# First chunk of a fused transformer block: keys formed ahead of values, values summed on GpSimd, and a new work order

## The chip, the cores and the metric

One NeuronCore of one Trainium2 chip runs one launch of the kernel. The metric is the device time of that launch in microseconds (us). The engines are named as the profile names them: PE (TensorE, matrix products; PEld is its weight load), DVE (VectorE), ACT (ScalarE), POOL (GpSimd) and SP (SyncE, which issues most DMAs).

## The reference

An input x of 2048 tokens by 256 features goes through three residual branches: half a top-1 gated attention, a gated linear recurrence with a skip matrix, and half the same attention again (same weights).

```python
def _L0_ffn_ref(x, W_gate, W_qkv):          # used twice, on _layernorm(x)
    gating = jax.nn.softmax(x @ W_gate.T, axis=-1)          # 16 heads
    idx = jnp.argmax(gating, axis=-1)
    indicator = jax.nn.one_hot(idx, H, dtype=gating.dtype)
    gating_top1 = indicator * jnp.max(gating, axis=-1, keepdims=True)
    q, k, v = jnp.split(x @ W_qkv.T, 3, axis=-1)
    k_shared = jnp.einsum('bth,bthd->btd', indicator, k)    # one key of 16 per token
    v_shared = jnp.einsum('bth,bthd->btd', gating_top1, v)  # one value of 16 per token
    att = jnp.einsum('bhqd,bkd->bhqk', q, k_shared) * (1.0 / math.sqrt(hd))
    att = softmax(causal(att))
    return jnp.einsum('bhqk,bkd->bhqd', att, v_shared)      # 16 heads
x = x + 0.5 * _L0_ffn_ref(_layernorm(x), ...)
x = x + _L0_attn_ref(_layernorm(x), ...)    # gates, a scan over time, W_out, W_skip
x = x + 0.5 * _L0_ffn_ref(_layernorm(x), ...)
```

## The kernel before

**Tiling.** The 2048 tokens are four chunks of 512 tokens (four tiles of 128). An attention *unit* is one layer, one chunk of queries and one group of four heads: 32 units in all, 320 *steps* of one key tile each. In a step PE forms the scores of four heads against 128 keys (`qk`, L1703), ACT takes the exponential (L1191), POOL masks the diagonal tile (L911), and PE multiplies with the shared values (`pv`, L1715). Before a unit may start, the largest score of each query is needed. It is found apart: PE forms the scores the other way round in *maximum banks* (`max`, L1680), DVE or ACT reduce them (L1406, L1409, L1175), POOL joins them (L930 to L933), PE turns the result into a row (`row`, L1671), ACT evicts it and SP sends it into the query tile by DMA (L830).

**Side work.** For each chunk a list named `prepare` gives the layer norm (`stats` on DVE, `norm` on POOL), the turned tokens (`turn`), the gate scores (`gate`), the top-1 choice (`pick`), the query products (`q`, sent through DRAM by `qout` and `qin`), key and value products (`kv`) and their sum over the chosen head (`choose`), the packed keys (`kpack`), their transposes (`keys`), and differences of keys (`dpack`, `dkeys`). The recurrence branch and the splitting of weights into two f16 parts (`bias`, `size`, `scale`, `split`) are side work too.

**First chunk.** For chunk 0 of layer 0, DVE multiplies each 128x512 bank of keys and values with the pick (L1370) and reduces it over the heads (L1377). Four such pairs, then ACT copies the values (L1122) and packs the keys (L1124), POOL finishes the packing (L969, L970), and PE transposes (L1627). In the other chunks POOL sums the products by halving (L955, L957).

**Order.** Each engine runs its part of one list, `ORDER`, in that order, and semaphores do the rest. The list begins with `FIRST_WORK`, written out; after that a string of digits, `PICKS`, says which of six queues gives the next item (scores, sums, maxima, ends, rows, side work). The string was found by a search over a planner, the class `Clock`, whose constants `WEIGHT`, `KEEPS` and others cost each item. A letter in the string is a group of *spare matmuls*: products of a constant whose result nobody reads (L1518 into a free bank, L1521 adding zeros to the sums), there to keep TensorE active. PE takes one of eight PSUM banks for each item and waits until its last reader is done (`bank_free`).

Of the kernel before, what the change touches and what calls it, by code (L numbers as in the profile page):

```python
# [142 lines left out]
def branch(c):  # L143
# [18 lines left out]
RINGED = {"weights", "scale", "wgate", "range", "bias", "turn", "gate", "kv", "q", "keys", "gates", "skip", "rec", "fin", "row", "max",  # L162
# [6 lines left out]
    "bias": (400, [("DVE", 200), ("POOL", 3500)]),  # L169
# [21 lines left out]
STRETCH, KEEPS, WAKES = 3413.3, 1843.0, 1480.0  # L191
# [12 lines left out]
def weights(e, past):  # L204
# [59 lines left out]
class Clock:  # L264
# [155 lines left out]
    "5522222222222255225255542255020252225055012222050422a525522220100111202225340221205150022122051122201002214223",  # L420
    "22221112023022222020222210220122221112222224322220020522022222222010220122201100221540010201025011202223500122",
    "202255555511510550222n0b01202b22022102201222222515122222452225553022555550225225222205500025005222210010115514",
    "02220152202212022252211022223202225522201022a52220102201522022101200221222252055555022154222222112222020555022",
    "32220525522201220205122020122015220220102220102202102222010220142022221220222122220211222022230220010202202102",
    "02211022201202201202220102220140222012222012222222102222022112202023020102022015005511022120220120220120222010",
    "222014202222120502212222a5222221100223220555222220122220522012220102120502212222050221022201220502505222220122",
    "05220412022252201022212202215122220530220122522201022021102022102220515500102022102225012022012205222201200252",
    "22100222120202142220522555022552205522202122550221122222252003122001220112222050221002210202215522500212220a50",
    "20522120022155005120222102201205502214202222522221202555222221122222225552023022052025255222201500225050022510",
# [122 lines left out]
def macaron_block(nc, x, gamma, beta, w_in, b_in, w_out, b_out, w_skip, b_skip, w_gate, w_qkv, out):  # L552
# [6 lines left out]
    with ctx:  # L559
# [1205 lines left out]
```

## Time and profile before

| | before |
|---|---|
| median of 3 runs | 843.93 us (842.96 to 843.97) |
| time of the profiled execution | 842.89 us |
| its span, first to last instruction | 841.2 us |
| PE busy | 805.8 us, 96% |
| DVE busy | 732.1 us, 87% |
| ACT busy | 710.9 us, 85% |
| POOL busy | 307.4 us, 37% |
| mean granted TensorE clock | 0.984 of full speed |

The profiled execution took 842.89 us, 1.7 us more than its span; the rest is around the first and the last instruction. Busy time is the union of an engine's records. Matmuls overlap in the record, so a busy PE need not be at its peak. The granted clock is 1.00 at 2.4 GHz and 0.50 at 1.2 GHz.

### The profile page before, as it was taken

The numbers are of one execution on the slowest core, as the hardware profiler recorded it, in microseconds if no ns is written. First come the engines' busy times: TensorE is split into PE (matmuls) and PEld (weight loads), VectorE is DVE, ScalarE is ACT, GpSimd is POOL, SyncE is SP. The second block draws the span as 40 slices with busy tenths as digits, with TensorE's granted clock in tenths as the row PEclk, the third lists the DMA queues.
The fourth block names the chain that finished last, engine by engine and source line by source line (L and its number), as shares of the span: only waits on it lengthen the run. The fifth ranks groups of instructions, "written<-read, shape, count | busy, mean of one in ns | idle before, by whom it ended". The sixth has DMA issues, their size and how long they took to land.

```text
span 841.2 us, 18837 instructions
## 1 busy us (share of the span) xinstructions
PE 805.8 (96%) x6403; PEld 283.5 (34%) x6403; DVE 732.1 (87%) x2315; ACT 710.9 (85%) x1117; POOL 307.4 (37%) x600
## 2 busy tenths in 40 slices
PE   8999899999999999999999999999999999999997
PEld 6433433333223332324333443332223333222221
DVE  5889799899999999999749996999999899999810
ACT  1149697979999899797989998899988998999996
POOL 3236424733113433246546258441234353011010
PEclk9999699999999999999999999999999999999999
DMA  6110000101000000200020001000001100000000
GB/s 191 61 59 7 2 2 20 47 14 53 2 2 2 1 2 2 64 1 2 2 64 2 2 12 54 3 1 26 3 2 34 33 27 27 2 2 2 1 1 26
DMA packets 20253, 17.99 MB, mean 21 GB/s; under 512 B 4144, under 2 KB 20160, under 8 KB 20160
## 3 DMA queue, kind: packets, MB, share of 16 engines
q1 hardware_dynamic: 19072, 15.74, 6.2%
q8 instruction: 52, 0.85, 0.4%
q10 hardware_dynamic: 1088, 1.07, 0.4%
q14 instruction: 41, 0.34, 0.1%
HBM read 10.24 MB, written 6.29 MB: 20 GB/s over the span
## 4 chain that ended last, share of the span: by engine, by line
PE 65%; DVE 13%; ACT 12%; issue 8%; POOL 1%; DMA 1%; SPq 0%; POOLq 0%; ACTq 0%; DVEq 0%
PE ps L1715 22%; PE ps L1680 14%; PE ps L1703 12%; ACT probs L1191 8%; DVE ps L1409 7%; ACT relu L1175 3%; PE ps L1598 3%; DVE mxp L1406 2%; PE ps L1646 2%; PE ps L1613 2%; DVE mxp L1409 1%; PE ps L1603 1%; PE ps L1653 1%; PE ps L1570 1%; PE ps L1618 1%
## 5 line engine op out<-in xcount | busy, mean ns | idle before, releaser
L1191 ACT ACTIVATE probs<-ps 128x1024 f32<-128x1024 f32 (+4 forms) x750 | 545.9, 807 | 53.7 <-PE ps L1703 49.1
L1715 PE MATMUL ps<-probs,v_l 128*32 128x512 f32 (+3 forms) x2560 | 298.5, 546 | 2.4 <-POOL probs L911 1.7
L1406 DVE TENSOR_REDUCE mxp<-ps 128x1 f32<-128x512 f32 x384 | 240.9, 684 | 9.8 <-PE ps L1680 5.9
L1409 DVE CUSTOM_DVE_ANT_0 ps<-ps,mask 128x384 f32<-128x384 f32 (+3 forms) x512 | 233.4, 525 | 15.7 <-PE ps L1680 14.7
L1703 PE MATMUL ps<-q_t,k_tl 50*128 50x512 f16 (+3 forms) x1280 | 225.6, 353 | 13.5 <-DMA q_t<-m_row 4.2
L1680 PE MATMUL ps<-k_tl,q_t 48*128 48x512 f16 (+3 forms) x1152 | 224.5, 336 | 4.4 <-DVE mxp L1409 1.2
L911 POOL TENSOR_SCALAR_AFFINE_SELECT probs<-probs 128x256 f32<-128x256 f32 (+1 forms) x192 | 91.7, 488 | 209.7 <-ACT probs L1191 208.6
L1409 DVE CUSTOM_DVE_ANT_0 ps<-ps,relu 128x256 f32<-128x256 f32 (+1 forms) x256 | 136.2, 587 | 8.1 <-PE ps L1680 7.0
L1680 PEld LDWEIGHTS ps<-k_tl,q_t 48*128 48x128 f16 x1152 | 70.5, 94 | 153.1 <-DVE mxp L1406 46.5
L1703 PEld LDWEIGHTS ps<-q_t,k_tl 50*128 50x128 f16 x1280 | 61.9, 94 | 175.2 <-ACT probs L1191 90.8
L1175 ACT ACTIVATE relu<-ps 128x512 f32<-128x512 f32 x192 | 107.3, 626 | 8.5 <-PE ps L1680 7.8
L1409 DVE DVE_READ_ACCUMULATOR2_ANT mxp<- 128x1 f32 x768 | 108.3, 141 | 0.0
L1715 PEld LDWEIGHTS ps<-probs,v_l 128*32 128x32 f32 x2560 | 53.6, 108 | 88.4 <-issue 74.4
L930 POOL TENSOR_SCALAR mxs<-mxf 128x16 f32<-128x16 f32 x32 | 8.1, 254 | 143.1 <-DVE mxf L1419 142.9
L917 POOL TENSOR_TENSOR x_sb<-x_sb,y_att 128x256 f32<-128x256 f32 x32 | 23.4, 730 | 54.6 <-DVE y_att L1432 54.3
L955 POOL TENSOR_TENSOR prod<-prod 128x512 f32<-128x512 f32 (+2 forms) x42 | 34.5, 820 | 22.7 <-DVE prod L1370 20.5
L1428 DVE RECIPROCAL rec<-ps 128x16 f32<-128x16 f32 x32 | 8.1, 252 | 39.8 <-PE ps L1689 39.8
L1680 PE MATMUL ps<-kd_tl,q_t 48*128 48x512 f16 x128 | 36.4, 382 | 1.8 <-DVE mxp L1409 1.0
L1598 PE MATMUL ps<-wqkv_x,ut_x 128*128 128x512 f16 x144 | 34.6, 380 | 0.1
L1370 DVE TENSOR_TENSOR prod<-ps,pick 128x512 f32<-128x512 f32 x32 | 22.0, 686 | 5.2 <-PE ps L1598 3.8
L876 POOL TENSOR_SCALAR u<-x_sb,rstd,shift 128x256 f32<-128x256 f32 x48 | 26.0, 555 | 1.1
L865 POOL TENSOR_TENSOR rstd<-var,half 128x4 f32<-128x4 f32 x12 | 12.5, 1038 | 35.2 <-DVE neg L1255 35.2
(183 smaller groups left out, 633.6 us busy)
## 6 DMA issues: line engine op xcount, KB each, us to landing
q_t<-q_scratch SPq DMA_DIRECT2D x96, 64.0 KB, 2.2
q_scratch<-q_part SPq DMA_DIRECT2D x16, 256.0 KB, 2.2
out_dram<-x_sb SPq DMA_DIRECT2D x4, 512.0 KB, 3.2
x_sb<-in_L_attn_x_dram SPq DMA_DIRECT2D x3, 512.0 KB, 5.1
q_t<-m_row SPq DMA_DIRECT2D x64, 4.0 KB
wqkv_n<-in_L_ffn_W_qkv_dram ACTq DMA_DIRECT2D x1, 768.0 KB, 5.7
w_in_sb<-in_L_attn_W_in_dram SPq DMA_DIRECT2D x1, 384.0 KB, 5.5
x_sb<-in_L_attn_x_dram ACTq DMA_DIRECT2D x1, 256.0 KB, 3.7
```

Source lines behind the costliest of these rows:

```text
L876: last = g_.tensor_scalar(u[:, t, :], x_sb[:, TC * c + t, :], rstd[:, t:t + 1], shift[:, t:t + 1], ALU.mult, ALU.add)
L911: g_.affine_select(out=pr, in_=pr, compare_op=ALU.is_ge, fill=0.0, base=0, pattern=[[0, n], [1, P]], channel_multiplier=-1).then_inc(s_msk, 1)
L917: g_.tensor_tensor(xs, xs, y_att[:, :, :].rearrange("p (i h) d -> p i (h d)", h=GH), op=ALU.add).then_inc(s_xa, 1)
L955: own(g_.tensor_tensor(pairs[:, :, 0:m], pairs[:, :, 0:m], pairs[:, :, m:2 * m], op=ALU.add))
L1175: a_.activation(relu[:, n % RELU_BUFS, :], bank_of(e), ACT.Relu).then_inc(s_ra, 1)
L1191: last = a_.activation(out[:, done:done + banks], scores, ACT.Exp, scale=SCALE / LIFT ** 2)
L1406: last = v_.tensor_reduce(to, scores, axis=AX, op=ALU.max)
L1409: last = v_.tensor_tensor_reduce(scores, scores, added, 1.0, LOWEST, ALU.add, ALU.max, accum_out=to)
L1598: last = mm(bank[:, :], ut_x[:, dc, a, t * P:(t + 1) * P], wqkv_x[:, b, dc, D:3 * D], start=n == 0, stop=n == 3 * DC - 1)
L1680: last = mm(bank[:, col:col + w], q_rows(ROWS_X, c, g, hh, i * P, P), keys, start=True, stop=True)
L1703: last = mm(ps[:, BANK[e][n % 2], col:col + w], k_cols(ROWS_XM, hh, l, kt, P), q_rows(ROWS_XM, c, g, hh, P * i, QW - P * i), start=True, s ...
L1715: last = mm(out_bank[VW * hh:VW * hh + VW, P * i:QW], v_l[:, l, kt, :], probs[:, s % NB, hh, P * i:QW], start=j == 0, stop=j == key_tiles( ...
```

## The change

In the first chunk of layer 0 alone, `kv` and `choose` are replaced. Keys come first: four products of 256 columns (`kk`), each multiplied and reduced on DVE at half the former width. Then the keys are packed (`kpack`), and only then are the pick's weights formed (`weigh`), and two products of two value tiles each (`vv`) multiplied on DVE. POOL sums the values by halving (`vsum`) and ACT copies them (`vpack`). The norm of this chunk is shared: POOL takes tiles 0 and 1, ACT tiles 2 and 3. The planner's cost of `bias` and its `KEEPS` are raised, and the whole string `PICKS` is new. Everything past the first chunk computes the same items in another order.

```diff
+OPENING = [("pick", 0, 0), ("q", 0, 0, 0), ("kk", 0, 0, 0), ("kk", 0, 0, 1), ("qout", 0, 0, 0), ("kk", 0, 0, 2), ("kk", 0, 0, 3),
+           ("q", 0, 0, 1), ("qin", 0, 0, 0), ("kpack", 0, 0), ("weigh", 0, 0), ("vv", 0, 0, 0), ("vv", 0, 0, 1), ("qout", 0, 0, 1),
+           ("keys", 0, 0), ("vsum", 0, 0), ("vpack", 0, 0), ("qin", 0, 0, 1), ("dpack", 0, 0), ("dkeys", 0, 0)]
...
-    + [("turn", 0, 0, 0), ("range", 0), ("turn", 0, 0, 1), ("range", 1), ("gate", 0, 0)] \
-    + prepare(0, 0)[5:]
+    + [("turn", 0, 0, 0), ("range", 0), ("turn", 0, 0, 1), ("range", 1), ("gate", 0, 0)] + OPENING
...
-    "bias": (400, [("DVE", 200), ("POOL", 3500)]),
+    "bias": (1300, [("DVE", 200), ("POOL", 3500)]),
...
-STRETCH, KEEPS, WAKES = 3413.3, 1843.0, 1480.0
+STRETCH, KEEPS, WAKES = 3413.3, 2400.0, 1480.0
...
 PICKS = (
-    "5522222222222255225255542255020252225055012222050422a525522220100111202225340221205150022122051122201002214223",
+    "522aaa22ba2252aba225a5aa22222b522225a4552505a022252525a50014222052205252250210a2012201122a45022211022515200212",
...
-                for t in range(TC):
+                for t in range(TC if k else 2):
                     last = g_.tensor_scalar(u[:, t, :], x_sb[:, TC * c + t, :], rstd[:, t:t + 1], shift[:, t:t + 1],
...
+            def values_sum():
+                pool.wait_ge(s_rd, FREED["vv", 0, 0, 1])
+                values = prod[:, :, D:2 * D]
+                m = D // 2
+                while m > HD:
+                    own(g_.tensor_tensor(values[:, :, 0:m], values[:, :, 0:m], values[:, :, m:2 * m], op=ALU.add))
+                    m //= 2
+                g_.tensor_tensor(kv[:, :, HD:2 * HD], values[:, :, 0:HD], values[:, :, HD:2 * HD], op=ALU.add)\
+                    .then_inc(s_vsum, 1)
...
+            def norm_half():
+                act.wait_ge(s_std, 1)
+                for t in range(2, TC):
+                    last = a_.activation(u[:, t, :], x_sb[:, t, :], ACT.Identity, bias=shift[:, t:t + 1],
+                                         scale=rstd[:, t:t + 1])
+                last.then_inc(s_half0, 1)
+            def values_in():
+                act.wait_ge(s_vsum, 1)
+                a_.activation(v_l[:, 0, 0:TC, 0:HD], kv[:, :, HD:2 * HD], ACT.Copy).then_inc(s_vpack, 1)
...
+                elif kind == "kk":
+                    t = e[3]
+                    dve.wait_ge(s_fill, filled(e))
+                    v_.tensor_tensor(prod[:, t, 0:D].rearrange("p (h d) -> p h d", d=HD),
+                                     bank_of(e)[:, 0:D].rearrange("p (h d) -> p h d", d=HD),
+                                     pick[:, t, 0, :].unsqueeze(2).to_broadcast([P, H, HD]), op=ALU.mult).then_inc(s_rd, 1)
+                    dve.wait_ge(s_rd, FREED[e])
+                    last = v_.tensor_reduce(kv[:, t, 0:HD], prod[:, t, 0:D].rearrange("p (h d) -> p d h", h=H), axis=AX, op=ALU.add)
+                    if t == TC - 1:
+                        last.then_inc(s_kv, 1)
+                elif kind == "vv":
+                    two = slice(2 * e[3], 2 * e[3] + 2)
+                    dve.wait_ge(s_fill, filled(e))
+                    v_.tensor_tensor(prod[:, two, D:2 * D].rearrange("p t (h d) -> p t h d", d=HD),
+                                     bank_of(e)[:, :].rearrange("p (t h d) -> p t h d", t=2, d=HD),
+                                     pick[:, two, 1, :].unsqueeze(3).to_broadcast([P, 2, H, HD]), op=ALU.mult).then_inc(s_rd, 1)
```

**PE, from the gate of the first chunk to the first maximum bank.** L1608 is the gate, L1618 `q`, L1613 `kv`, L1627 `keys` and then `dkeys`, L1518 the spare matmuls, L1680 the maxima. Before:

```order
L1608 MATMUL ps<-wg_t,ut 128x16 x8
L1618 MATMUL ps<-ut,wqkv_t 128x512 x2
L1613 MATMUL ps<-wqkv_t,ut 128x512 x2
L1618 MATMUL ps<-ut,wqkv_t 128x512 x2
L1613 MATMUL ps<-wqkv_t,ut 128x512 x6
L1518 MATMUL ps<-ident 128x512 x17
L1627 MATMUL ps<-ident_h,k_rows 128x128 x4
L1518 MATMUL ps<-ident 128x512 x7
L1627 MATMUL ps<-ident_h,k_rows 128x128 x2
L1680 MATMUL ps<-k_tl,q_t 128x512 x2
```

With the change the lines read L1673, L1694 (`q`), L1678 (`kk`), L1684 (`vv`), L1703 (`keys`, then `dkeys`), L1582 and L1756:

```order
L1673 MATMUL ps<-wg_t,ut 128x16 x8
L1694 MATMUL ps<-ut,wqkv_t 128x512 x2
L1678 MATMUL ps<-wqkv_t,ut 128x256 x8
L1694 MATMUL ps<-ut,wqkv_t 128x512 x2
L1684 MATMUL ps<-wqkv_t,ut 128x256 x8
L1703 MATMUL ps<-ident_h,k_rows 128x128 x4
L1582 MATMUL ps<-ident 128x512 x22
L1703 MATMUL ps<-ident_h,k_rows 128x128 x2
L1756 MATMUL ps<-k_tl,q_t 128x512 x2
```

The keys' transposes now follow the products at once, and the 22 spare matmuls stand between them and the transposes of the differences, which still come ahead of the first maximum.

**POOL, the same place.** Before, the packed keys (L969, L970), the differences (L973, L974, L984), and the next norm (L865):

```order
L969 TENSOR_SCALAR k_in<-kv,w_mul 128x64
L970 TENSOR_TENSOR k_rows<-k_in,k_rows 128x8x16
L973 COPY k_first<-k_in 128x64
L974 TENSOR_TENSOR k_diff<-k_in 128x32
L984 TENSOR_TENSOR k_rows<-k_diff,k_rows 128x4x16
L865 TENSOR_TENSOR rstd<-var,half 128x4
```

With the change:

```order
L1000 TENSOR_SCALAR k_in<-kv,w_mul 128x64
L1001 TENSOR_TENSOR k_rows<-k_in,k_rows 128x8x16
L1004 COPY k_first<-k_in 128x64
L1005 TENSOR_TENSOR k_diff<-k_in 128x32
L988 TENSOR_TENSOR prod<-prod 128x4x128
L988 TENSOR_TENSOR prod<-prod 128x4x64
L988 TENSOR_TENSOR prod<-prod 128x4x32
L990 TENSOR_TENSOR kv<-prod 128x4x16
L1015 TENSOR_TENSOR k_rows<-k_diff,k_rows 128x4x16
L884 TENSOR_TENSOR rstd<-var,half 128x4
```

The four additions of the value sum stand ahead of the last step of the key differences and of the next norm.

**PE, around the first row.** L1671 is the row of unit 0, L1703 its first scores. Before:

```order
L1608 MATMUL ps<-wg_t,ut 128x16 x8
L1680 MATMUL ps<-k_tl,q_t 128x384
L1680 MATMUL ps<-k_tl,q_t 128x128
L1618 MATMUL ps<-ut,wqkv_t 128x512 x2
L1613 MATMUL ps<-wqkv_t,ut 128x512 x2
L1671 MATMUL ps<-ident_h,mx 32x128
L1680 MATMUL ps<-k_tl,q_t 128x512 x2
L1618 MATMUL ps<-ut,wqkv_t 128x512 x2
L1703 MATMUL ps<-q_t,k_tl 128x512 x2
```

With the change (L1747 is the row, L1689 `kv`, L1779 the scores):

```order
L1582 MATMUL ps<-ident 128x512 x2
L1673 MATMUL ps<-wg_t,ut 128x16 x8
L1756 MATMUL ps<-k_tl,q_t 128x384
L1756 MATMUL ps<-k_tl,q_t 128x128
L1756 MATMUL ps<-k_tl,q_t 128x512 x2
L1756 MATMUL ps<-k_tl,q_t 128x384
L1756 MATMUL ps<-k_tl,q_t 128x128
L1582 MATMUL ps<-ident 128x512
L1747 MATMUL ps<-ident_h,mx 32x128
L1694 MATMUL ps<-ut,wqkv_t 128x512 x2
L1689 MATMUL ps<-wqkv_t,ut 128x512 x2
L1756 MATMUL ps<-k_tl,q_t 128x384
```

The row now stands ahead of the products of chunk 1 (L1694, L1689), and spare matmuls are spread among the maxima.

## Rows read from the trace of the kernel before

**Rows 1.** The page: span, and the granted clock in 40 slices
```profile
span 841.2 us, 18837 instructions
...
PEclk9999699999999999999999999999999999999999
```

**Rows 2.** Busy time in five stretches: us, engines, PEclk, DMA share, GB/s
```profile
32.60:60.00 27.40, 24.91 (x117) 11.80 (x115) 23.59 (x94) 8.70 (x14) 8.38 (x20) 0.88 0.11 35
80.00:125.00 45.00, 41.05 (x327) 16.28 (x324) 39.08 (x162) 35.20 (x60) 15.44 (x31) 0.81 0.01 2
125.00:760.00 635.00, 617.82 (x5090) 210.06 (x5090) 588.22 (x1820) 574.52 (x912) 250.23 (x449) 1.00 0.06 17
760.00:780.00 20.00, 18.80 (x136) 5.02 (x137) 18.34 (x56) 18.36 (x32) 4.16 (x10) 0.91 0.01 2
780.00:841.20 61.20, 53.92 (x408) 13.09 (x404) 22.26 (x42) 51.58 (x65) 4.90 (x11) 1.00 0.03 10
```

**Rows 3.** The same view of the four stretches of low clock
```profile
38.50:46.00 7.50, 7.50 (x23) 4.69 (x23) 6.38 (x32) 0.81 (x2) 0.70 (x3) 0.54 0.00 0
83.00:87.00 4.00, 4.00 (x31) 1.05 (x28) 3.40 (x19) 2.81 (x6) 1.15 (x3) 0.57 0.01 4
93.00:107.50 14.50, 13.82 (x93) 6.30 (x90) 10.19 (x52) 9.25 (x17) 7.04 (x12) 0.53 0.00 1
776.00:779.50 3.50, 3.50 (x24) 0.56 (x19) 2.56 (x7) 2.60 (x5) 1.56 (x3) 0.51 0.00 0
```

**Rows 4.** Timeline of the first 34 us: start us, us, engine, line, operation
```profile
10.21 2.10 PE L1518 MATMUL ps<-ident 128*128 128x512 f16 x9
...
12.15 0.60 PE L1575 MATMUL ps<-ident,u 128*128 128x128 f32 x4
...
14.51 1.96 PE L1608 MATMUL ps<-wg_t,ut 128*128 128x16 f32 x16
...
19.13 0.75 DVE L1389 SCALAR_TENSOR_TENSOR q_part<-ps,w_mul,q_part 128x512 f16<-128x512 f32 x1 [0.20 <-ACT q_part L1113]
...
21.55 5.31 PE L1613 MATMUL ps<-wqkv_t,ut 128*128 128x512 f32 x12
...
26.70 3.83 PE L1518 MATMUL ps<-ident 128*128 128x512 f16 x17
...
28.95 0.49 ACT L1124 ACTIVATE k_rows<-kv,w_mul 128x256 f16<-128x256 f32 x1
...
30.65 0.38 PE L1627 MATMUL ps<-ident_h,k_rows 128*128 128x128 f16 x4
...
31.94 0.30 POOL L984 TENSOR_TENSOR k_rows<-k_diff,k_rows 128x64 f16<-128x64 f32 x1 [0.93 <-ACT k_rows L1133]
...
32.60 1.04 PE L1680 MATMUL ps<-k_tl,q_t 48*128 48x512 f16 x12
```

**Rows 5.** All instructions on tile prod: count, ns min/median/max, first and last start
```profile
L955 POOL TENSOR_TENSOR prod<-prod x42: 451/731/1282, 56.5 to 657.4; 128x512 f32<-128x512 f32 x14, 128x256 f32<-128x256 f32 x14, 128x128 f32<-128x128 f32 x14
L1370 DVE TENSOR_TENSOR prod<-ps,pick x32: 678/686/692, 20.0 to 654.5; 128x512 f32<-128x512 f32 x32
L957 POOL TENSOR_TENSOR kv<-prod x14: 318/322/327, 59.2 to 658.0; 128x64 f32<-128x64 f32 x14
L1377 DVE TENSOR_REDUCE kv<-prod x4: 1008/1010/1011, 20.8 to 27.7; 128x32 f32<-128x512 f32 x4
```

**Rows 6.** Timeline of PE from 38.1 to 51 us, columns as in rows 4
```profile
38.15 3.00 PE L1608 MATMUL ps<-wg_t,ut 128*128 128x16 f32 x16 [0.35 <-ACT ut L1082]
...
41.62 3.78 PE L1618 MATMUL ps<-ut,wqkv_t 128*128 128x512 f32 x4
45.20 2.08 PE L1613 MATMUL ps<-wqkv_t,ut 128*128 128x512 f32 x4
47.21 0.23 PE L1671 MATMUL ps<-ident_h,mx 128*32 128x128 f16 x1
...
50.51 0.39 PE L1703 MATMUL ps<-q_t,k_tl 50*128 50x512 f16 x2 [0.83 <-DMA q_t<-m_row]
```

More of the change, by code:

```diff
@@ L160 @@
     + branch(1) + prepare(1, 1) + branch(2) + prepare(1, 2) + branch(3) + prepare(1, 3)
-RINGED = {"weights", "scale", "wgate", "range", "bias", "turn", "gate", "kv", "q", "keys", "gates", "skip", "rec", "fin", "row", "max",
+RINGED = {"weights", "scale", "wgate", "range", "bias", "turn", "gate", "kv", "kk", "vv", "q", "keys", "gates", "skip", "rec", "fin", "row", "max",
           "dkeys"}
@@ L217, in weights @@
         return HALVED[e[0]][0], "full", HALVED[e[0]][1]
+    if e[0] == "pick" and e[1:3] == (0, 0):
+        return 0, "full", [("DVE", 800)]
+    if e[0] in ("kk", "vv"):
+        return (860, "full", [("DVE", 930)]) if e[0] == "kk" else (1720, "full", [("DVE", 605)])
+    if e[0] in ("weigh", "vsum", "vpack"):
+        return 0, "full", [{"weigh": ("DVE", 750), "vsum": ("POOL", 2950), "vpack": ("ACT", 160)}[e[0]]]
     if e[0] == "choose" and e[1:3] in POOLED:
@@ L239, in needs @@
     k = e[0]
+    if k in ("kk", "vv"):
+        return [("turn", 0, 0, 1)]
+    if k in ("weigh", "vsum", "vpack"):
+        return [{"weigh": ("pick", 0, 0), "vsum": ("vv", 0, 0, 1), "vpack": ("vsum", 0, 0)}[k]]
+    if e == ("kpack", 0, 0):
+        return [("kk", 0, 0, TC - 1)]
     if k in ("norm", "halve", "turn", "gate", "pick", "q", "qout", "kv", "choose", "kpack", "keys"):
@@ L425 @@
[L425 to L429, printed above, removed]
@@ L1482, in _ @@
                     ranges(e)
-                elif e[0] in ("gate", "pick", "kv", "q") or (e[0] == "choose" and e[1:3] not in POOLED):
+                elif e[0] in ("gate", "pick", "weigh", "kk", "vv", "kv", "q"):
                     preparation(e)
@@ L1608, in preparation @@
                             last = mm(bank[:, t * H:(t + 1) * H], ut[:, dc, t * P:(t + 1) * P], wg_t[:, dc, :],
+                                      start=dc == 0, stop=dc == DC - 1)
+                elif kind == "kk":
+                    t = e[3]
+                    for dc in range(DC):
+                        last = mm(bank[:, 0:D], ut[:, dc, t * P:(t + 1) * P], wqkv_t[:, dc, D:2 * D],
+                                  start=dc == 0, stop=dc == DC - 1)
+                elif kind == "vv":
+                    for n in range(2):
+                        t = 2 * e[3] + n
+                        for dc in range(DC):
+                            last = mm(bank[:, n * D:(n + 1) * D], ut[:, dc, t * P:(t + 1) * P], wqkv_t[:, dc, 2 * D:3 * D],
                                       start=dc == 0, stop=dc == DC - 1)
@@ L1733, in _ @@
                     turn(e)
-                elif e[0] in ("gate", "kv", "q", "keys", "dkeys"):
+                elif e[0] in ("gate", "kv", "kk", "vv", "q", "keys", "dkeys"):
                     preparation(e)
```

95 lines of the change are left out of this document (55 added, 40 removed).

## The prediction

> **What bounds the kernel now.** I read the page first. The span is 841.2 us, and the granted clock is below full in one of 40 slices only [rows 1]. Then a table by stretch [rows 2]. From 125 to 760 us PE is busy 617.8 of 635 us: it is the bound there, with 17.2 us idle to be won. From 32.6 to 60 us DVE is busy 23.6 of 27.4 us, and from 80 to 125 us 39.1 of 45. In these two stretches the clock is down too, at 0.88 and 0.81. A finer table finds four low stretches [rows 3], at a mean of 0.51 to 0.57, so nearly all at 1.2 GHz: 7.5, 4, 14.5 and 3.5 us. The sum of length times missing share is 7.5 x 0.46 + 4 x 0.43 + 14.5 x 0.47 + 3.5 x 0.49 = 3.5 + 1.7 + 6.8 + 1.7 = 13.7 us, the most that a full clock could return if PE were the only bound.
>
> The timeline of the opening [rows 4] gives the chain to the first maximum bank at 32.60 us: gate, products until 26.86, DVE's last reduction (it starts at 27.7 and takes 1.01 [rows 5]), ACT's packing at 28.95, transposes at 30.65, POOL's last step of the differences at 31.94, their transposes, first maximum. The timeline of PE after that [rows 6] shows the row of unit 0 only at 47.21, behind gate, query and key products at low clock, and the first scores at 50.51.
>
> **The change, part by part.** Durations are from the profiled execution (842.89 us, span 841.2). It lies 1.0 us under the median of 843.93, so I take the difference that I work out from the median.
>
> *Norm shared by POOL and ACT: 0.* The first turn issues at 12.15 us directly behind nine spare matmuls that began at 10.21 [rows 4]; the order still has nine. If that cover went, the gain would be at most the 1.94 us between these starts, so the range takes -1.9 to +0.5.
>
> *Keys first.* PE streams as many columns as before: 8 products of 256 and 4 of 512 for the query, then 8 of 256. It should still be done near 26.9 us [rows 4]. DVE ends the first query part at 19.13 + 0.75 = 19.9. One product and reduction of 512 wide cost 0.69 + 1.01 = 1.70 us [rows 5]. At half the width they cost between 0.85 (all by width) and 1.70 (all fixed); I take 1.0, near the lower end as the width is what halves. Four make 4.0, so the keys are summed at 23.9. ACT evicts the second query part, then packs: 0.49, near 24.8; POOL is through near 25.7. The transposes wait for PE's products and issue at 27.0 in place of 30.65. That is 3.6 us earlier, and **I count it as 0**: the next useful thing on PE is the transposes of the differences, and those have moved behind the value sum.
>
> *Values on POOL.* DVE's last value product can't start before 27.0 (PE's end and a handover) and takes 0.69 at 512 wide: 27.7. POOL's four additions at the same widths as L955 and L957 take 1.27 + 0.73 + 0.46 + 0.32 = 2.8 us [rows 5]: 30.6. Queued behind them on POOL is L1015, and ahead of its input on ACT is the copy of the values. ACT's two copies (bounded by the 0.49 of L1124 each, by nothing below; I take 0.55 for both), POOL's 0.30, and four handovers of about 0.1 give 31.9, then 0.3 of transposes: first maximum at 32.2 in place of 32.60. Term: **-0.4**, range -1.9 to +1. The 22 spare matmuls ahead of it take 22 x 3.83/17 = 5.0 us from 27.3, so until 32.2: they fit exactly and would hide an earlier sum. Here the Trainium skill speaks against the change. "GPSIMD Engine Reference", section "Engine selection", gives elementwise additions to VectorE and calls GpSimd about 2x slower for two inputs. The trace agrees in direction: 2.8 us for the values of four tiles against at most 4 x 1.01 for keys and values on DVE. By that rule the sum would stay on DVE; its last reduction at half width would then take about 0.5 us in place of 2.8 after the last product, and the first maximum could come 2.3 us sooner. The sum above does not use it.
>
> *From the first maximum to the first attention.* DVE needs the same ten banks before the join. With the change 18 spare matmuls stand where one stood, among the maxima. They are 18 x 0.225 = 4.1 us of PE, against its idle time of 27.4 - 24.9 = 2.5 us plus the 3.5 us that full clock frees. The gate should take 1.96 in place of 3.00, the first query product some 1.9 in place of 3.78 [rows 4, 6]. The row leaves PE's queue ahead of both products, at about 42 us in place of 47.21; 3.3 us lie between row and scores (47.21 to 50.51), and PE fills them with 3.8 us of products. So first scores near 46, some 4 us earlier, though with one query product (1.9 us) still owed. DVE bounds what stays: its idle time is 27.4 - 23.6 = 3.8 us. Term: **-3.0**, range 0 to -3.8.
>
> *80 to 125 us.* If the clock stays up there, 8.5 us of PE time return (3.4 x 0.5 and 13.65 x 0.5). DVE's idle time, 45 - 39.1 = 5.9 us, caps it, and the stretch is a chain too: bias, size, scales, splits, then the turn of chunk 2. Both orders keep a like number of spare matmuls over it (18 and 19, at the splits), and the new one has 11 more ahead of them in place of none. Nearer to half of the cap: **-2.5**, range 0 to -5.9.
>
> *760 to 780 us.* Clock 0.91: 1.7 us at most, ACT idle 1.6. **-0.8**, range 0 to -1.6.
>
> *The other spare matmuls.* In all 146 stand in place of 71. From 125 to 760 us there are some 36 more, where the clock was already full and nothing is to be had for them: 36 x 0.225 = 8.1 us if each stands where PE is busy, 0 if each stands in its 17.2 us of idle time. The order spreads them by ones and twos at starts of units, where PE waits for rows: I take **+1.5**. In the last unit 26 stand in place of 14, beside 61.2 - 53.9 = 7.3 us of idle PE: 0.
>
> *The rest of the new order:* same work. What can be won is within the 17.2 us of idle PE, what can be lost has no bound in a row. 0, range -3 to +4.
>
> Sum: -0.4 - 3.0 - 2.5 - 0.8 + 1.5 = -5.2. I round down to -5, since the row's 4 us was read with PE free to take it: 843.93 - 5 = **839 us**.
>
> **The rivals.**
> 1. *Everything returns.* DVE's 3.8 and 5.9, ACT's 1.6 at the end: -11.3, so 832.6. For it: the row leaves 5 us earlier, spare matmuls ahead of the low stretches. Against it: the splitting chain is serial, and DVE's idle time is never all won. 0.12.
> 2. *The low clock only moves.* It falls somewhere else once the order has changed, so 80 to 125 and 776 return nothing; the opening gives 1.5, the spare matmuls take it: 843.9. For it: the old order held spare matmuls for the same purpose, 18 of them in units 4 and 5, and the clock fell four times all the same [rows 3]. Against it: those 18 stood behind the low stretches, not ahead, and the new order has 11 ahead of unit 5 where the old had none. 0.17.
> 3. *Slower: spare matmuls on a busy PE.* From 125 to 760 us PE has 97% busy records. If all 36 stand on that path they cost 8.1; with 3.0 from the opening and no clock returned the time is 849.0. It decides from 28 of the 36 on if all three gains come (6.3 / 0.225), from 14 on if the opening alone does. Against it: they stand next to waits. 0.12.
>
> **How the numbers follow.** About 0.2%, 1.7 us, is what a measurement of this kernel can tell. My forecast has 0.59, its own range 835 to 842.5. Leaving out the lower half of rival 1 and the upper part of rival 3 gives 833.5 to 846. Faster: 0.57 of the forecast's 0.59, and 0.12: 0.69. Same: 0.02 and most of rival 2: 0.17. Slower: rival 3 and an edge of rival 2: 0.14.
>
> **What would show it.** Right: transposes of the keys near 27 us, POOL's value sum 27.8 to 30.6, first maximum at 32 to 32.6, row of unit 0 near 42, first scores near 46; clock above 0.95 in 32.6 to 60; fewer or shorter low stretches after 80. Wrong: first maximum by 30 (then the value sum was no bound), row behind 45, a low stretch of 10 us or more between 60 and 125, or PE's idle time from 125 to 760 far from 17 us less the time of the added spare matmuls.

## The result, and the profile after

The changed kernel takes **830.68 us** (median of 4 runs, 829.87 to 830.99) against 843.44 us for the kernel before on the same chip (4 runs): a ratio of 0.9852 (95% interval 0.9837 to 0.9868). The forecast was 839, so 12.8 us went where 5 were expected, and the time lies below the range. The profiled executions are 842.89 and 830.62 us, 12.27 apart; the readings below use these two.

The page of the kernel after: span, busy time, and the granted clock in 40 slices.

```profile
span 828.9 us, 18895 instructions
...
PE 810.2 (98%) x6494; PEld 284.1 (34%) x6494; DVE 728.0 (88%) x2317; ACT 707.3 (85%) x1013; POOL 311.5 (38%) x602
...
PEclk9999899999999999999999999999999999999999
```

PE is busy 4.4 us longer than before (805.8) in a span 12.3 us shorter, so its idle time fell from 35.4 to 18.7 us, by 16.7. The added spare matmuls, 75 of about 0.22 us, fill 16 of these. PE's other work then takes some 12 us less, and about 8 of the 12 are the clock: the share of the clock that is missing, times the span, is 13.7 us before and 5.6 us after.

The same kernel by stretch, at the cuts of [rows 2] with its own end (us, then PE, PEld, DVE, ACT and POOL busy with counts, granted clock, DMA share, GB/s), and its one low stretch behind the opening:

```profile
32.60:60.00 27.40, 27.34 (x151) 11.55 (x150) 26.73 (x107) 9.37 (x16) 10.65 (x23) 1.00 0.17 50
80.00:125.00 45.00, 43.20 (x354) 15.41 (x354) 40.08 (x166) 37.65 (x54) 19.00 (x36) 0.92 0.01 2
125.00:760.00 635.00, 625.70 (x5157) 210.26 (x5157) 592.35 (x1826) 575.65 (x830) 249.29 (x447) 1.00 0.06 17
760.00:780.00 20.00, 19.96 (x159) 5.74 (x159) 19.30 (x52) 18.23 (x25) 3.54 (x7) 1.00 0.00 1
780.00:828.90 48.90, 44.75 (x330) 11.29 (x327) 10.67 (x20) 41.09 (x47) 4.98 (x11) 0.99 0.04 12
...
93.20:100.00 6.80, 6.77 (x37) 1.74 (x33) 4.84 (x24) 4.03 (x7) 5.37 (x9) 0.57 0.00 0
```

The clock stays full from 32.6 to 60 us, the 18.5 us of low clock after 80 us [rows 3] have shrunk to 6.8, and the low stretch at 776 us is gone. The last row is 12.3 us shorter than its counterpart.

Timeline of the opening, kernel after, against [rows 4] and [rows 6] (start us, us, engine, line, operation):

```profile
26.98 0.39 PE L1703 MATMUL ps<-ident_h,k_rows 128*128 128x128 f16 x4
...
27.20 4.91 PE L1582 MATMUL ps<-ident 128*128 128x512 f16 x22
...
27.95 2.61 POOL L988 TENSOR_TENSOR prod<-prod 128x512 f32<-128x512 f32 x3 [1.57 <-DVE prod L1434]
...
30.63 0.32 POOL L990 TENSOR_TENSOR kv<-prod 128x64 f32<-128x64 f32 x1
...
32.17 0.39 PE L1756 MATMUL ps<-k_tl,q_t 48*128 48x512 f16 x2
...
41.47 0.23 PE L1747 MATMUL ps<-ident_h,mx 128*32 128x128 f16 x1
...
45.84 0.39 PE L1779 MATMUL ps<-q_t,k_tl 50*128 50x512 f16 x2
```

These are close to the times of the prediction (27.0, 27.8 to 30.6, 32.2). The row of unit 0 is at 41.47 us on PE in place of 47.21, the first scores at 45.84 in place of 50.51. But this execution has a stretch of low clock ahead of them, and another execution of the same kernel (c1, below) has none. The window from 15 to 19.5 us in this execution, then in c1:

```profile
15.00:19.50 4.50, 4.50 (x11) 2.46 (x11) 2.29 (x11) 0.94 (x2) 0.00 (x0) 0.62 0.44 138
```

```profile
15.00:19.50 4.50, 4.50 (x20) 3.26 (x20) 3.17 (x13) 0.94 (x2) 0.10 (x1) 1.00 0.52 180
```

and two rows of c1's timeline:

```profile
25.65 0.39 PE L1703 MATMUL ps<-ident_h,k_rows 128*128 128x128 f16 x4
...
30.85 0.39 PE L1756 MATMUL ps<-k_tl,q_t 48*128 48x512 f16 x2
```

In c1 the transposes of the keys come 1.3 us earlier and the first maximum at 30.85 us, 1.75 us earlier than in the kernel before.

**Where the 12.3 us come from** is told by markers that every kernel has once per unit: ACT's copy of a unit's sums (tile o_sb), the *end* of the unit here, and ACT's eviction of a unit's row (tile m_row), the *row*. Their starts in us, read from the timelines of the profiled executions (labels as in the experiments below):

```
kernel                      row 0   end 5   end 10  end 27  row 31  end 31   row 31 - end 27   end 31 - row 31
before                      47.48  137.39   271.20  700.68  803.70  834.88        103.0              31.2
after                       42.84  131.86   267.39  695.47  790.95  822.62         95.5              31.7
c1 changed kernel again     41.51  130.26   267.39  695.46  790.96  822.63         95.5              31.7
e1 old opening, new order   43.59  134.06   272.37  700.43  795.93  827.61         95.5              31.7
e2 new opening, old order   46.66  136.70   270.69  700.10  803.73  834.91        103.6              31.2
h1 old order to unit 5      46.74  136.52   272.69  701.03  796.51  828.19         95.5              31.7
h2 old order to unit 27     48.33  137.37   271.58  701.23  803.79  835.46        102.6              31.7
h3 new order to unit 27     41.75  130.66   267.68  695.73  797.77  829.08        102.0              31.3
e8 no spares, units 6-29    43.07  132.08   270.42  699.96  795.42  827.10         95.5              31.7
e5 norm scale later         41.75  130.69   263.02  691.10  786.57  818.24         95.5              31.7
```

To the end of unit 5 the change returns 5.5 us, from there to unit 27 it gives back 0.3, and in the last four units it returns **7.05**. In c1 the split is another, 7.1 us and 1.9 given back, with the same sum at unit 27. The last column is nearly the same in all kernels: once row 31 is there, the end follows 31.2 to 31.7 us later (32.3 in e4 alone). Both orders leave the same 18 steps of sums and nearly as many scores behind that row, and no maxima. So the gain of the tail lies in when the last row is ready. In every profile the last reduction of a maximum bank ends 1.5 us before ACT evicts that row. The windows from the end of unit 27 to row 31, and from there on, before:

```profile
700.70:803.70 103.00, 98.14 (x755) 26.21 (x755) 96.08 (x237) 97.80 (x152) 12.52 (x30) 0.98 0.02 7
803.70:834.90 31.20, 30.03 (x226) 7.01 (x225) 0.68 (x2) 28.66 (x34) 3.50 (x7) 1.00 0.01 1
```

and after:

```profile
695.50:791.00 95.50, 94.41 (x742) 25.65 (x741) 90.68 (x213) 90.84 (x120) 12.30 (x29) 1.00 0.02 7
791.00:822.60 31.60, 31.09 (x235) 7.57 (x232) 0.69 (x2) 30.31 (x35) 3.57 (x7) 1.00 0.01 2
```

In the first window DVE has 5.4 us less to do (96.08 to 90.68, 24 instructions fewer): by the end of unit 27 the new order has finished 8 more maximum banks (157 left in place of 165, at about 0.68 us each). ACT has 7.0 us less to do in 32 instructions fewer, and the forms of its exponentials tell most of why. PE is idle for 4.9 us before and 1.1 after, and the low clock of the kernel before (0.98) is worth 1.7 us at most. Groups of ACT's instructions over the whole run by shape, before (count | busy us, mean ns | idle before):

```profile
L1191 ACT ACTIVATE probs<-ps 128x1024 f32<-128x1024 f32 x336 | 334.2, 1040 | 34.5 <-PE ps L1703 31.1
L1191 ACT ACTIVATE probs<-ps 128x512 f32<-128x512 f32 x306 | 166.9, 612 | 12.6 <-PE ps L1703 11.5
```

and after:

```profile
L1238 ACT ACTIVATE probs<-ps 128x1024 f32<-128x1024 f32 x421 | 413.7, 1039 | 43.7 <-PE ps L1779 40.5
...
L1238 ACT ACTIVATE probs<-ps 128x512 f32<-128x512 f32 x149 | 82.5, 609 | 11.8 <-PE ps L1779 10.8
```

The scores of two heads fill two banks. Where these are neighbours in PSUM, one instruction of 1024 columns serves both (1040 ns); where they are not, ACT needs two of 512 (2 x 612 ns), 0.18 us more. The new order finds neighbours far oftener: 68 exponentials are *split* in place of 174, and in units 28 to 30 8 in place of 35. The prediction didn't look at either.

One thing is worse. Timeline of the kernel after near 246 us (in brackets the idle time before, and who ended it):

```profile
246.76 0.16 DVE L1306 TENSOR_SCALAR neg<-mv 128x4 f32<-128x4 f32 x1
247.00 1.04 POOL L884 TENSOR_TENSOR rstd<-var,half 128x4 f32<-128x4 f32 x1 [2.19 <-DVE neg L1306]
248.12 0.20 POOL L885 TENSOR_TENSOR shift<-neg,rstd 128x4 f32<-128x4 f32 x1
248.27 0.64 POOL L930 TENSOR_SCALAR_AFFINE_SELECT probs<-probs 128x512 f32<-128x512 f32 x1
...
249.05 0.43 PE L1791 MATMUL ps<-probs,v_l 128*32 128x128 f32 x8 [3.06 <-POOL probs L930]
```

POOL waits 2.19 us for DVE's statistics to form a norm's scale, and the mask of a diagonal tile, long ready, stands behind it in POOL's queue. PE waits for that mask 3.06 us. This stall is new here; the kernel before has one like it of 1.25 us at 622 us.

### The profile page after: what moved, and what is told of

Its sections match the earlier page's. It is cut to its first block, busy times and chain, and to the rows that moved or that the text cites. A ratio compares the mean times of both kernels' runs of the same rounds, so it can differ in the third digit from the quotient of the medians.

```text
span 828.9 us, 18895 instructions
## 1 busy us (share of the span) xinstructions
PE 810.2 (98%) x6494; PEld 284.1 (34%) x6494; DVE 728.0 (88%) x2317; ACT 707.3 (85%) x1013; POOL 311.5 (38%) x602
## 4 chain that ended last, share of the span: by engine, by line
PE 69%; DVE 18%; issue 5%; ACT 4%; POOL 2%; DMA 1%; SPq 0%; ACTq 0%; POOLq 0%; DVEq 0%
PE ps L1791 24%; PE ps L1756 15%; PE ps L1779 13%; DVE ps L1473 9%; DVE mxp L1470 3%; PE ps L1582 3%; PE ps L1663 2%; ACT probs L1238 2%; DVE mxp L1473 2%; PE ps L1722 2%; PE ps L1729 1%; PE ps L1668 1%; PE ps L1765 1%; PE ps L1736 1%; PE ps L1694 1%
## 5 line engine op out<-in xcount | busy, mean ns | idle before, releaser
L1238 ACT ACTIVATE probs<-ps 128x1024 f32<-128x1024 f32 (+2 forms) x644 | 539.8, 906 | 60.8 <-PE ps L1779 56.2
L1791 PE MATMUL ps<-probs,v_l 128*32 128x512 f32 (+3 forms) x2560 | 295.5, 541 | 3.8 <-POOL probs L930 3.4
L1779 PE MATMUL ps<-q_t,k_tl 50*128 50x512 f16 (+3 forms) x1280 | 220.2, 351 | 5.1 <-DMA q_t<-m_row 1.5
L1756 PE MATMUL ps<-k_tl,q_t 48*128 48x512 f16 (+3 forms) x1152 | 222.3, 334 | 1.9 <-ACT probs L1238 0.3
L1779 PEld LDWEIGHTS ps<-q_t,k_tl 50*128 50x128 f16 x1280 | 61.6, 93 | 179.2 <-ACT probs L1238 88.0
L1756 PEld LDWEIGHTS ps<-k_tl,q_t 48*128 48x128 f16 x1152 | 69.8, 94 | 139.2 <-DVE mxp L1473 37.5
L1492 DVE RECIPROCAL rec<-ps 128x16 f32<-128x16 f32 x32 | 8.2, 255 | 42.5 <-PE ps L1765 42.3
L1582 PE MATMUL ps<-ident 128*128 128x512 f16 x132 | 39.7, 386 | 0.0
L1756 PE MATMUL ps<-kd_tl,q_t 48*128 48x512 f16 x128 | 34.2, 382 | 0.3 <-ACT probs L1238 0.2
L961 POOL TENSOR_TENSOR u_x<-u,u_x 128x512 f16<-128x512 f32 x20 | 23.2, 1159 | 1.7
```

The costliest lines, as they stand in the source:

```text
L1238: last = a_.activation(out[:, done:done + banks], scores, ACT.Exp, scale=SCALE / LIFT ** 2)
L1582: mm(bank_of(e), some[:, 0:P], stream, start=True, stop=True)
L1756: last = mm(bank[:, col:col + w], q_rows(ROWS_X, c, g, hh, i * P, P), keys, start=True, stop=True)
L1779: last = mm(ps[:, BANK[e][n % 2], col:col + w], k_cols(ROWS_XM, hh, l, kt, P), q_rows(ROWS_XM, c, g, hh, P * i, QW - P * i), start=True, s ...
L1791: last = mm(out_bank[VW * hh:VW * hh + VW, P * i:QW], v_l[:, l, kt, :], probs[:, s % NB, hh, P * i:QW], start=j == 0, stop=j == key_tiles( ...
```

## The experiments

Each is timed against the kernel before on its own chip. A time alone is the median of its runs. Unit ends are those of the profiled execution.

### Opening and order apart

```diff
# e1: the kernel before with the new order
+PICKS, KEEPS 2400, cost of bias 1300    (as in the change)
# e2: the changed kernel with the old order
+PICKS, KEEPS 1843, cost of bias 400     (as before)
```

> The kernel before with the new string PICKS (and the planner's constants that go with it), the old first chunk. Theory A (the new order of the body brings nearly everything: fuller clock, maxima ahead of need, fewer split score banks): 830 to 833 us, 10 to 13 under the kernel before. Theory B (the new first chunk is needed for it): 836 or more. The new opening reached its first maximum only 0.4 us earlier, so A expects no more than 1.5 us between this kernel and the changed one.

> The changed kernel with the old string PICKS and the old constants of the planner. Theory A (the order of the body brings it): 842 to 845 us, as before. Theory B (the opening brings it): 836 or less. The clock should still fall near 39 and 93 us under A.

e1: 834.66 us (831.83 to 835.79), ratio 0.9897 (0.9868 to 0.9926). e2: 843.1, ratio 1.0014 (1.0 to 1.0028). The new opening alone is worth nothing, the order alone some 8 us, both 12.8. In e2 row 0 comes at 46.66 us, since the clock falls all the same, and for longer than before [rows 3]. Window of e2:

```profile
34.00:46.00 12.00, 11.30 (x38) 7.40 (x37) 9.72 (x46) 2.14 (x4) 0.93 (x4) 0.57 0.00 0
```

e1 falls between the two theories. Most of the earlier row 0 is there without the new opening (43.59). What e1 lacks of the changed kernel is 2.2 us at unit 5, with low clock from 42.5 to 46 us, and 2.8 more by unit 10, with low clock behind the stall of 246 us; its tail is the same as after. The changed kernel has such a fall behind the stall in c1 too, so these 2.8 us are not shown to be the opening's.

### The order cut at units

The string was cut where unit 5 or unit 27 ends; what was left followed in the other order, all with the new opening. In h2 one spare matmul is left out as well, and the eight maximum banks that the old order has not yet done stand at the head of what is left.

```diff
# h1: old order up to ("oev", 5), the rest in new order
# h2: old order up to ("oev", 27), the rest in new order
# h3: new order up to ("oev", 27), the rest in old order
```

> New opening, old order of the body until the sums of unit 5 are out (near 137 us), then what is left in the new order. Theory A (by the times at which each unit's sums leave, the new order gains 4.8 us by there and the rest behind): 830.7 + 4.8 = 835.5. Theory B (the spare matmuls that hold the clock in the first 60 us matter little, the gain is all later): 832 or less.

> New opening, old order until the sums of unit 27 are out (near 700 us), then what is left in the new order (one spare matmul left out). The changed kernel gains 7.0 us in the last four units. Theory L (it is a lead: the new order has 8 more maximum banks done by then, 5.4 us of DVE, and their lack starves the last units): the gain is mostly absent here, 840 or more. Theory T (it is how the last four units are ordered): 843.1 - 7.0 = 836.

> The changed kernel, but what is left after the sums of unit 27 in the old order. Theory L (lead of maxima): the lead is kept at the cut, so at most 834. Theory T (ordering of the last units): 830.7 + 7.0 = 837.7.

h1: 838.27 (836.18 to 840.92), ratio 0.9938 (0.9915 to 0.996). h2: 842.31, ratio 0.9983 (0.9973 to 0.9993). h3: 836.85, ratio 0.9917 (0.9896 to 0.9938). h1's median is 2.8 us above its expectation; its profiled execution, the fastest of six, took 836.18, so most of that excess is in executions that no profile shows. It comes to unit 27 0.35 us later than the kernel before and still ends 6.7 us earlier: the tail's gain does not need an earlier start. But h2, whose last four units run in the new order without the lead in maxima, gains almost nothing, and h3, which has the lead and 5 us in hand at unit 27 and ends in the old order, loses 6.2 of the tail's gain again. By the expectations h2 speaks for the lead and h3 (836.85, near the 837.7 of theory T) for the order of the last units. The window from unit 27 to row 31 of h3, then of h2:

```profile
695.70:797.80 102.10, 95.88 (x740) 25.51 (x740) 91.45 (x214) 95.66 (x150) 12.14 (x29) 0.98 0.02 6
```

```profile
701.20:803.80 102.60, 99.58 (x756) 27.11 (x754) 96.17 (x237) 94.16 (x128) 12.81 (x30) 0.97 0.02 7
```

h2 has DVE's 96.2 us of before; h3 has the 91.4 of after, but 150 ACT instructions in place of 120, and DVE idle for 10.7 us in place of 4.8. So the tail's gain takes both, the order up to unit 27 and the order behind it. That the first gives it by the eight maximum banks done ahead is likely, not shown: h2 falls 6.6 us behind the changed kernel within unit 28 and 0.5 more after, and in that unit its clock is low too, which is worth 3.4 us at most:

```profile
705.00:712.30 7.30, 7.13 (x33) 2.31 (x34) 5.74 (x17) 3.92 (x8) 2.54 (x5) 0.53 0.14 45
```

h3 has 1.7 us of missing clock at most, in a stretch 6.6 us longer than that of after.

### Splits of the exponential

```diff
# e4: every fourth pair apart, 165 splits in place of 68
-        if n == 2 and late > 0:
+        if n == 2 and (late > 0 or self.pairs % 4 == 0):
# e7: pairs apart in units 28 to 30 alone, 41 splits in place of 8; one spare matmul left out
+            self.bank[e] = self.choose(t, 2, 28 <= STEPS[e[1]][0] <= 30 and (e[1] + e[2]) % 4 == 0)
# h4: h3, but in units 28 on a split only if neighbours would cost over 800 ns; 3 in place of 36
# e10: the same threshold everywhere, in the kernel of e5 below; 12 in place of 68
-        if n == 2 and late > 0:
+        if n == 2 and late > 800:
```

> The changed kernel with every fourth pair of score banks forced apart, so 165 exponentials are taken in two halves in place of 68 (the kernel before had 174). The order is unchanged. A split costs ACT 2 x 612 - 1040 = 184 ns by the trace, so 97 more cost ACT 18 us if all are of full width. If ACT's extra instructions matter for the end: 3 us or more slower, 834 to 845. If ACT has room everywhere: within 1 us of 830.7.

> The changed kernel with 41 split exponentials in units 28 to 30 in place of 8 (35 in the kernel before, 36 in the one with the old tail), same order. If the splits are why the old tail leaves DVE idle for 10.6 us and takes 102 us from the sums of unit 27 to the last row in place of 95.5: 4 us or more slower than the changed kernel. If they are a symptom of the old order: 0.5 to 2 us slower, ACT's own extra work (33 x 0.184 = 6 us beside 4.7 us of idle ACT).

> The kernel with the old order of the last four units (836.85 us), with banks chosen so that 3 exponentials of these units are split in place of 36. If the splits are the whole loss of the old tail: about 831. If they are half, as 3.5 of 6.2 us by the forced splits suggests: 833 to 834.5. If waiting for adjacent banks costs as much as a split: 836 to 838.

> The same, with banks chosen so that 12 exponentials of the whole run are split in place of 68: 56 x 0.184 = 10 us less work on ACT, against PE's waits for adjacent banks. If ACT's extra work is felt as in the forced splits (3.5 us for 33, 2.2 us for 97 spread ones): 1 to 3 us faster than its yardstick. If PE's waits take it: same or slower.

In these four the planner's choice of one bank moves the banks of other items too, so each shows the splits together with that.

e4: 832.89 (831.92 to 834.13), ratio 0.9888, again between the theories: 97 more splits cost 2.2 us, an eighth of their 97 x 0.18 = 17.8 us of ACT. Only 10 of them fall in units 28 to 30. e7: 835.17 (834.13 to 836.09), ratio 0.9913. Its ends of units 27 to 31 lie 0.5, 1.8, 2.7, 3.5 and 3.5 us behind those of the changed kernel: 33 splits at the end cost 3.5 us, where their ACT time is 6.1. Window of e7 from unit 27 to row 31:

```profile
695.90:794.50 98.60, 95.08 (x741) 25.18 (x742) 91.06 (x213) 93.13 (x150) 12.30 (x29) 1.00 0.02 7
```

DVE is idle for 7.5 us in place of 4.8. One reading is that the maxima need the same eight banks, which come free later; no run tests it. But having fewer splits is no gain in itself: h4 takes 842.2 us, ratio 1.0018, 5 more than h3, and e10 842.65, ratio 1.0002, 15.9 more than the same kernel without the threshold on its chip (c2, below). From 125 to 760 us, at full clock, PE is idle for 19.1 us in e10 and 6.1 in e5. So waiting for neighbours costs more than splitting. In h4's tail the clock is low for 6.9 us as well, so its 5 us are not all this wait.

### Spare matmuls

```diff
# e3: all spare matmuls behind the opening's list taken out (113)
+ORDER = ORDER[:len(FIRST_WORK) + 3] + [e for e in ORDER[len(FIRST_WORK) + 3:] if e[0] != "warm"]
# e8: only those between the ends of units 5 and 29 (37)
+_a, _b = ORDER.index(("oev", 5)), ORDER.index(("oev", 29))
+ORDER = ORDER[:_a] + [e for e in ORDER[_a:_b] if e[0] != "warm"] + ORDER[_b:]
# e9: only those from the first maximum to the end of unit 5 (48)
+_a, _b = ORDER.index(("max", 0, 0)), ORDER.index(("oev", 5))
```

> The changed kernel without any spare matmul behind the transposes of the first chunk (113 of 146 gone), all else in the same order and the same banks. If the spare matmuls bring the gain by holding the clock: the mean clock falls from 0.993 to 0.97 or less and the time rises by 4 us or more, to 835 or above. If they cost time on PE (the rival of the prediction): it falls, by up to 5 us. If they only fill idle time and the clock needs them in a few places: within 2 us of 830.7.

> The changed kernel without its 37 spare matmuls between the sums of unit 5 and of unit 29. The prediction priced them at +1.5 us of cost: then 829.2. If they fill PE's waits and nothing else: 830.7. If they keep the clock up here as well: a stretch of low clock appears behind 137 us and the time rises by 1 to 4 us.

> The changed kernel without its spare matmuls between the first maximum and the sums of unit 5 (132 us). The prediction's terms of 3.0 and 2.5 us rest on the clock that these hold. If so: the clock falls again near 39 us and near 93 us, and the time is 834 to 836. If the order alone brings these terms: within 1 us of 831.

e3: 835.77 (834.86 to 837.54), ratio 0.9923, mean clock 0.979. e8: 834.96 (834.49 to 835.43), ratio 0.9905. e9: 835.82 (832.57 to 837.52), ratio 0.9921. Against the changed kernel's 830.68 they are 4.3 to 5.1 us slower; e8 is 3.4 us slower than c1 (831.57), which ran on its chip. e8 matters most, for the prediction gave its 37 a cost of 1.5 us. Windows of e8:

```profile
214.00:220.00 6.00, 5.32 (x30) 1.35 (x32) 5.52 (x17) 5.30 (x9) 2.95 (x6) 0.77 0.01 3
248.00:256.00 8.00, 5.50 (x38) 1.25 (x38) 3.17 (x9) 3.38 (x5) 7.24 (x11) 0.79 0.00 1
660.00:672.00 12.00, 11.30 (x74) 2.79 (x69) 10.48 (x33) 10.38 (x19) 0.00 (x0) 0.86 0.01 1
```

The clock falls three times where the profiles of both kernels had it full, and the units come 1.2, 1.6 and 1.5 us later. The second fall isn't the lack of spare matmuls alone: c1, which has them all, falls at the same place (last section) and loses 1.6 us there. So 2.7 us are left for the other two. Where e8's clock is full it gains nothing without them: it stays 0.2 us behind from unit 5 to unit 8, and 2.9 to 3.0 us behind from unit 11 to 22. So they cost nothing either.

The stretch from 38 to 46 us in e9, then in the changed kernel:

```profile
38.00:46.00 8.00, 8.00 (x28) 5.44 (x29) 7.55 (x34) 0.65 (x3) 0.69 (x3) 0.55 0.00 1
```

```profile
38.00:46.00 8.00, 7.94 (x44) 4.25 (x40) 7.83 (x38) 1.20 (x4) 0.69 (x3) 1.00 0.00 1
```

e9 is 1.8 us behind the changed kernel at the end of unit 5 (133.68 against 131.86; 3.4 us behind c1). It is 4.4 us behind at unit 10 and 5.5 at unit 14. The second step comes with a low stretch behind the stall at 246 us, which c1 has half as long; for the last 1.1 us no low stretch is there and the cause stays open. Three windows of e9, the first two at the cuts of [rows 2]:

```profile
32.60:60.00 27.40, 26.30 (x118) 12.87 (x117) 24.47 (x98) 8.43 (x13) 8.71 (x20) 0.81 0.15 46
80.00:125.00 45.00, 39.30 (x343) 14.12 (x337) 41.48 (x174) 38.48 (x57) 17.99 (x34) 0.89 0.01 2
249.80:256.80 7.00, 5.98 (x30) 1.29 (x30) 2.52 (x5) 3.00 (x4) 6.43 (x11) 0.51 0.01 2
```

Up to unit 5 e9 misses as much clock as the kernel before, 11.9 us each of missing share times length, and still ends that unit 3.7 us earlier. So of the 5.5 us there the clock that these spare matmuls hold explains 1.8 (3.4 of 7.1, measured from c1), and 3.7 us come without it.

e3 also settles something on the tail. It has no spare matmul there; window from the end of unit 27 to row 31:

```profile
700.90:796.40 95.50, 93.05 (x736) 25.31 (x737) 90.71 (x214) 90.91 (x120) 12.32 (x29) 1.00 0.02 7
```

The stretch is as short as in the changed kernel and the clock is full. So the tail's gain doesn't come from its spare matmuls, and PE's 97% of busy records there do not need them.

### The stall at 246 us, and earlier maxima

```diff
# e5: POOL forms a norm's scale where the norm stands, not where the statistics stand
-                elif e[0] == "stats":
-                    stats_of(e)
                 elif e[0] == "norm":
+                    stats_of(("stats",) + e[1:])
                     norm(e)
# e6: e5, with the 22 spare matmuls out and the key differences behind ten maximum banks
+ORDER = [e for e in ORDER if e != ("dkeys", 0, 0) and e[:2] != ("warm", 2)]
+ORDER.insert(ORDER.index(("max", 0, 9)) + 1, ("dkeys", 0, 0))
```

> The changed kernel, with POOL forming each chunk's norm scale (power and product, L884 and L885) at the place of the norm and no longer at the place of the statistics. In the changed kernel every engine but POOL stands still from 246.8 to 249.0 us: a diagonal mask is queued on POOL behind the scale, which waits for DVE's statistics. If that stall is real time on the path: 3 us less, 827.7. If it is given back later (DVE or ACT bound): within 1 us of 830.7. If the later scale delays norms: slower.

> The kernel with the later norm scale (826.0 us), with the transposes of the first chunk's key differences and the 22 spare matmuls ahead of them taken from ahead of the first maximum: the transposes stand behind the tenth maximum bank, the spare matmuls are gone. If the value sum and the differences behind it were all that kept the first maximum from using the early keys (the reading of the prediction): DVE's first maximum starts near 30.2 us, behind its statistics, in place of 32.6, and if DVE's maxima set the end the time falls by 1 to 2.4 us, to 823.6 to 825. If the turn and gate of chunk 1 bind there instead, which wait for POOL's norm: the first scores keep their place near 45 us and the time is 826 within 1.

> The changed kernel itself once more, as the yardstick for the three kernels that run on the same chip beside it: 830 to 831.5 us. All theories agree.

> The kernel with the later norm scale again, as a yardstick: 826 to 827 us. It was 826.0 on another chip.

**e5 is the best kernel of all: 826.02 us** (825.53 to 826.25), ratio 0.9788 (0.9767 to 0.9809); again as c2: 826.76, ratio 0.982 (0.9803 to 0.9837). The changed kernel again, c1, on a third chip: 831.57, ratio 0.987 (0.9832 to 0.9909). The unit ends show the gain in place. Against c1, which like e5 has full clock in the opening, e5 is 0.4 us later at unit 9, 4.4 earlier at unit 10 and 4.4 earlier at the end. POOL in e5 and the same stretch by window:

```profile
242.66 1.77 POOL L930 TENSOR_SCALAR_AFFINE_SELECT probs<-probs 128x256 f32<-128x256 f32 x3
245.86 1.04 POOL L884 TENSOR_TENSOR rstd<-var,half 128x4 f32<-128x4 f32 x1 [1.43 <-DVE neg L1305]
```

```profile
246.00:252.00 6.00, 6.00 (x52) 1.67 (x50) 5.62 (x10) 5.68 (x7) 5.61 (x9) 1.00 0.01 3
```

The masks now come ahead of the scale, and PE is busy through the whole window.

e6: 827.43 (826.89 to 828.4), ratio 0.9818. DVE starts the first maximum at 29.23 us, 3.4 us earlier than in the changed kernel, yet row 0 comes at 42.28 us, against 41.75 in e5. Its row and a window behind the place of the removed matmuls:

```profile
29.23 0.69 DVE L1474 CUSTOM_DVE_ANT_0 ps<-ps,mask 128x512 f32<-128x512 f32 x1
```

```profile
32.00:36.00 4.00, 2.05 (x14) 1.27 (x13) 3.74 (x18) 0.60 (x1) 2.40 (x6) 0.90 0.01 2
```

An earlier first maximum is worth nothing in this form. That bears on the rule weighed in the prediction ("GPSIMD Engine Reference" of the Trainium skill, section "Engine selection", which gives such additions to VectorE). Its direction agrees with the trace: the value sum takes 3.0 us on POOL, and the four reductions of the same width for the keys take 4 x 0.58 = 2.3 us on DVE. But the 2.3 us that the prediction worked out for the first maximum would hardly have reached row 0. As the clock also dipped in e6, whether a start at 29 us can be used with spare matmuls placed otherwise stays open.

## Why the prediction was wrong

- **Norm shared: 0, keys first: 0, values on POOL: -0.4.** In the profiled execution the transposes of the keys came at 26.98 us for 27.0, the first maximum at 32.17 for 32.2. This agreement is partly luck. The first turn came 1.3 us earlier than before (10.87 for 12.15), which the prediction put at nothing, and a stretch of low clock from 15.6 to 19 us took it back. c1 has no such stretch, and its first maximum is at 30.85, 1.75 us earlier than before. It mattered little: e6 starts the maxima earlier still and gains nothing. The half-width pairs on DVE take about 1.0 us, as taken.
- **First maximum to first attention: -3.0, and 80 to 125 us: -2.5.** Right in sum: with the -0.4 they make -5.9, and unit 5 ends 5.5 us earlier (7.1 in c1). The mechanism was half right. The prediction had both come by the clock. The clock is full from 32.6 to 60 us and the row is early, as forecast, but e9 misses as much clock as the kernel before and has 3.7 of the 5.5 us all the same. The prediction named the earlier place of the row, yet priced it only together with full clock.
- **The other spare matmuls: +1.5, in the last unit 0.** Wrong in sign. PE's idle time from 125 to 760 us fell from 17.2 to 9.3 us, by about what the 36 take (8.1), and e8 shows that they cost nothing. What the prediction said of them, that "the clock was already full and nothing is to be had for them", fails: without 37 of them this order is 3.4 us slower than c1 on the same chip, with 2.7 us at two falls of the clock that no profile with them shows. Their value isn't a gain over the kernel before, whose order held the clock there without them; it is what keeps the new order from losing.
- **Rest of the new order: 0, 760 to 780 us: -0.8, and 0 for the last unit.** This is the step that failed. Units 6 to 27 gave back 0.3 us in all, and within that is a new stall of 3.06 us that e5 takes out with a gain of 4.4. But the last four units returned 7.05 us, where the terms allowed 0.8: some 2.4 by the end of unit 29, near 763 us, and 4.7 after. The working priced the low clock of one window, capped by ACT's idle time there, and took PE's 97% of busy records as the bound of the rest, so that "same work" in another order was worth nothing. What the runs show in its place: the end stands 31.2 to 31.7 us behind row 31, and row 31 came 7.5 us sooner after unit 27. The new order reaches unit 27 with 8 maximum banks more done (8 x 0.68 = 5.4 us of DVE), and keeps DVE and PE waiting less behind it. By h2 and h3 neither half of the order gives the tail's gain alone. The low clock of before is worth 1.7 of the 7.5 us at most, and the spare matmuls of the tail none (e3). Of the tail's own part, h3 shows 6.2 us; forced splits cost 3.5 us (e7), so splits may be up to that much of it. How the rest divides between the places of the maxima, the banks and the clock stays open.

Rival 1 named nearly the time (832.6) by another mechanism: it took back all of DVE's idle time in the opening and 1.6 us at the end. The first half came to 5.5 us of its 9.7, the end to 7.05. That its time was near is luck.

## What to carry to other kernels

Read the end by itself: take a late event that every kernel has (here the last row), and look whether the time from it to the end is fixed. If so, ask what that event waits for, also where an engine shows 97% busy. Compare two executions of the same kernel before an agreement to 0.1 us is called right. When an order is found anew, compare what it does to the forms of instructions and to work done ahead at a few cuts, since both move time that no single item of the difference shows. In an in-order queue look for an item that waits for a late input ahead of one that is ready and wanted: moving one such item gave some 4.5 us more.

## What was not expected of the hardware

- Few spare matmuls can hold the clock of a PE that already shows 98% busy records: 37 from unit 5 to unit 29, and without them two falls near 217 and 668 us, at 1.2 and 1.5 us (e8), that no profile with them has.
- The same kernel lowers the clock in different places in different executions. The changed kernel had a low stretch in the opening (0.62 from 15 to 19.5 us) and full clock behind the stall at 246 us. Its repeat c1 was 1.6 us ahead at unit 5 and showed low clock behind the stall, here by its window, and both end unit 10 at 267.39 us:

```profile
248.90:252.30 3.40, 3.40 (x15) 0.51 (x15) 2.05 (x4) 2.31 (x4) 3.17 (x6) 0.50 0.00 0
```

- One exponential over two neighbouring banks costs 1040 ns, two over single banks 1224 ns, so where PE's results land in PSUM is worth 0.18 us of ACT each time.
